# A vision tower's attention phase: scores one eighth of a unit earlier, and features gathered in the first six eighths

## The reference

```
h = einsum('bhid,oi,od->bho', x, weighted_sum, weight)
h = h + attn(layernorm(h))
h = h + ffn(layernorm(h))
```

```
h = ln(x, g1, beta1)
q = elu((h @ wq per head) @ proj) + 1
k = elu((h @ wk per head) @ proj) + 1
v = h @ wv
kv = kv + k_t v_t ; ksum = ksum + k_t        # over tokens
out_t = (q_t . kv) / (q_t . ksum + 1e-6)
x = x + out @ wo ; x = x + mlp(ln(x))
```

## Time and profile before

| | us |
|---|---|
| median of 3 runs | 2545.34 (2538.14 to 2553.37) |
| profiled execution | 2542.18 |
| its span | 2540.4 |
| PE busy | 2215.7 (87%) |
| VectorE busy | 1784.6 (70%) |
| ScalarE busy | 1524.6 (60%) |
| GpSimd busy | 1467.8 (58%) |

### The profile page before, as it was taken

The page is one execution under the profiler, slowest core; times in us unless marked ns, Lnnn a source line. Parts: engine busy times, 40 slices in busy tenths (PEclk is TensorE's granted clock), DMA queues, the critical chain, the costliest instruction groups (busy, mean ns, idle before and its releaser), DMA issues. The chain is left out here.

```text
span 2540.4 us, 64867 instructions
## 1 busy us (share of the span) xinstructions
PE 2215.7 (87%) x24112; PEld 1732.1 (68%) x24112; DVE 1784.6 (70%) x3983; ACT 1524.6 (60%) x2890; POOL 1467.8 (58%) x1449
## 2 busy tenths in 40 slices
PE   3799999999989899999999986799999999994764
PEld 2577777778778777777778775466666666662653
DVE  3477777777777777777777775478788887874443
ACT  3476676676766676667667664556566565651322
POOL 1466666575666666656657654035646555556676
PEclk8899999999999999999999998899999999997897
DMA  3344444344454343434433333111212111100775
GB/s 112 97 119 113 122 123 124 104 131 122 105 132 124 100 105 102 108 99 105 110 101 104 89 87 112 40 60 45 82 43 83 45 60 52 40 22 22 166 139 72
DMA packets 323208, 236.43 MB, mean 93 GB/s; under 512 B 40345, under 2 KB 288141, under 8 KB 322896
## 3 DMA queue, kind: packets, MB, share of 16 engines
q1 hardware_dynamic: 286640, 197.30, 28.6%
q0 software_dynamic: 23808, 21.74, 4.9%
q10 hardware_dynamic: 12448, 13.24, 1.6%
HBM read 73.32 MB, written 82.58 MB: 61 GB/s over the span
## 5 line engine op out<-in xcount | busy, mean ns | idle before, releaser
L965 POOL TENSOR_TENSOR lo<-z,hi 128x512 f16<-128x512 f32 x256 | 306.1, 1196 | 342.8 <-DVE hi L874 328.5
L1850 POOL DMA_INDIRECT slot_dram<-xt,slot_u x256 | 267.0, 1043 | 77.4 <-issue 77.4
L543 PE MATMUL pF<-nh,qk_h 128*128 128x256 f16 x1024 | 282.7, 276 | 7.5 <-DVE nl L862 4.4
L545 PE MATMUL pF<-nl,qk_h 128*128 128x256 f16 x1024 | 282.6, 276 | 0.0
L544 PE MATMUL pF<-nh,qk_l 128*128 128x256 f16 x1024 | 282.6, 276 | 0.0
L789 ACT ACTIVATE sh<-sm 128x512 f16<-128x512 f32 x256 | 159.5, 623 | 106.3 <-DVE sm L895 106.2
L984 POOL TENSOR_TENSOR kvl<-kvacc,kvh 128x260 f16<-128x260 f32 x192 | 157.4, 820 | 77.2 <-ACT kvh L820 77.1
L869 DVE SCALAR_TENSOR_TENSOR z<-pF,z 128x512 f32<-128x512 f32 x256 | 174.9, 683 | 24.6 <-ACT z L772 22.2
L768 ACT ACTIVATE z<-pF 128x512 f32<-128x512 f32 x256 | 150.4, 587 | 69.6 <-PE pF L545 69.6
L543 PE MATMUL pM<-xh,tok_h 128*128 128x256 f16 x512 | 141.3, 276 | 53.9 <-POOL xl L959 53.3
L895 DVE TENSOR_TENSOR sm<-pS,mask 128x512 f32<-128x512 f32 x256 | 174.5, 681 | 17.2 <-PE pS L629 16.9
(11 more groups left out here) (298 smaller groups left out, 8494.2 us busy)
## 6 DMA issues: line engine op xcount, KB each, us to landing
w_w<-in_x SPq DMA_DIRECT2D x128, 256.0 KB, 3.0
qdh<-hi SPq DMA_DIRECT2D x512, 64.0 KB, 2.1
qdl<-lo SPq DMA_DIRECT2D x512, 64.0 KB, 2.1
ks<-hi SPq DMA_DIRECT2D x256, 64.0 KB, 2.1
ks<-lo SPq DMA_DIRECT2D x256, 64.0 KB, 2.1
slot_dram<-blank ACTq DMA_DIRECT2D x8, 1360.0 KB, 7.1
xg<-slot_dram SPq DMA_DIRECT2D x40, 272.0 KB, 3.2
x_dram<-x SPq DMA_DIRECT2D x32, 256.0 KB, 2.4
```

Source lines behind the costliest of these rows:

```text
L543: pe.matmul(out, wh, mh, start=first, stop=False, skip_group_check=True)
L545: return pe.matmul(out, wh, ml, start=False, stop=last, skip_group_check=True)
L965: nc.gpsimd.tensor_tensor(lo[:, n % 2, :, :], z[:, units(w, FEATS, n) % ZS, :, :], hi[:, n % MOVES, :, :], ALU.subtract).then_inc(fl_ready, 1)
L1850: nc.gpsimd.indirect_dma_start(io["slot_dram"], bass.IndirectOffsetOnAxis(slot_u[:, i % XT, c, k:k + 1], 0), xt[:, i % XT, c, :], None, bo ...
```

## The change: the table of dense work and the place of the scores

Each quad is scored one eighth earlier: quads 0, 1, 2 of the next chunk stand at g = 1, 2, 3, and quad 3 of the present chunk at g = 0. Three quads, not two, are scored ahead of the first unit. In the table the features stand in s0, s1, s3, s4, s5 and the values in s6 and s7; the projection stays early in s2. Each inner tuple is an eighth, its first entry early, its second late.

```diff
-DENSE = ((("f", 0),), (("f", 1), ("f", 2)), (("p", 0), ("f", 3)), (("v", 0), ("v", 1)), (("f", 4),),
-         (("f", 5), ("f", 6)), (("f", 7), ("v", 2)), (("v", 3),))
+DENSE = ((("f", 0), ("f", 1)), (("f", 2),), (("p", 0),), (("f", 3), ("f", 4)), (("f", 5),),
+         (("f", 6), ("f", 7)), (("v", 0), ("v", 1)), (("v", 2), ("v", 3)))
...
-                    if g < 2:
-                        quad = (i, c, g + 2)
+
+                    if g == 0:
+                        quad = (i, c, 3)
                     elif c < CH - 1:
-                        quad = (i, c + 1, g - 2)
+                        quad = (i, c + 1, g - 1)
                     else:
-                        quad = None if last else (i + 1, 0, g - 2)
+                        quad = None if last else (i + 1, 0, g - 1)
...
-            for q in range(2):
+            for q in range(3):
                 step("scores", 0, 0, q)
                 step("scores_split", 0, 0, q)
```

## The result

The changed kernel takes 2708.06 us (median of 4 runs, 2706.14 to 2711.91) against 2548.79 for the kernel before (4 runs): ratio 1.0637, 95% interval 1.0614 to 1.0661. The direction was forecast, the size was not: +160 us where +100 was forecast, and the time lies above the range. The profiled execution took 2709.5 us, its span is 2707.8, and 163.5 us of the 167.4 by which the span grew lie between the first scores and the last projection (1465.2 us before, 1628.7 now). What comes behind that point takes 966 us before and 967 after. So the question stays inside the attention phase.

What follows compares the result with a forecast made beforehand. PE's work plus its waits were taken to bound the attention phase. New waits 183 plus 19 minus old waits 132 gave +70; with +30 for the clock, 2542 became 2642 us; 8-in-10 range 2550 to 2700.

Steps and rivals of the forecast that it cites:

- Part one: Before the outputs (pO): scoring quads 1 and 3 two eighths ahead removes all 57.1 us of PE's wait.
- The scores at s7: PE waits for f7 behind SyncE's queue of DMAs: 3.35 us per unit, bounds 0.9 and 4.3.
- mix 0: First mixing group, s4: new wait for xl 0 of 1.9 us every unit; above 2.4 if f3's lo is late.
- mix 2: Mixing group waiting for xl 2 behind f6's lo: new wait 1.25 us in odd halves, 0.1 in even ones.
- Rival A: The scores' wait doesn't grow, since the last feature's own chain decides; faster, 2455 or 2485 us; chance 12%.
- Var and the keys: Waits at var and the keys of s1, 0.3 us each, 19 us over 31 units; each between 0 and 1.4.
- The clock: PE's clock falls behind 18 of 31 waits for the scores, 1.65 us each: +30 us, bounds 0 and 51.
- all 31: Upper bound of the clock cost: a fall behind each of the 31 waits for the scores, 51 us.
- The window of the earlier trace with 0.81: Window around one of PE's longest waits for the scores, granted clock 0.81: that fall cost 1.5 us.
- the old 132: PE's old waits before outputs, mixing, scores and key transposes, 132.0 us, taken away entirely as the most the change can give.
- C: Rival: each of the 31 stalls drops the clock, 2663 us; 2708 with mix 0 and s7 at upper bounds; chance 22%.

Runs made afterwards that it cites:

- e6: The changed kernel with four of the eight DMAs of each query feature left out (scores wrong there); ratio 1.0065.
- e4: The changed kernel with SyncE issuing each input load behind the next feature's DMAs instead of ahead of them; ratio 1.0358.
- e3: The changed kernel with f4 early and f5 late in s4, so no late feature in s3; ratio 1.0627.
- e13: The changed kernel with the first input split of s3 (xh, xl 0, SyncE's load) ahead of GpSimd's sl of quad 2 and kvl; ratio 1.0491.
- after: The changed kernel itself, with both the earlier quads and the new feature table, against the kernel before; 2708.06 us, ratio 1.0637.
- e7: The kernel before (quads where they were) with the new table, but f4 early and f5 late in s4; ratio 0.9981.
- e5: The changed kernel with dummy matmuls filling PE's waits, 24 before the wait for f7 and 16 before mix 0; ratio 1.0540.
- e15: The kernel before with the new table, and in s3 and s7 the scores, their mask and their split moved ahead; ratio 0.9852.
- e1: The changed kernel with the table of before, so the earlier quads alone; ratio 1.0984.
- e8: As e7, with SyncE's input loads behind the next feature's DMAs too; ratio 0.9985.
- e9: The kernel before with the new table, and in s3 and s7 the scores' split ahead of the late dense group; ratio 0.9982.
- e16: The same kernel as e2, run again on another chip; ratio 0.9863.
- e2: The kernel before with the new feature table and the quads where they were; ratio 0.9861.

## Why the prediction was right in direction and wrong in size

**Part one, the outputs' 57 us go: right.** Their idle is 0.0.

**The scores at s7, forecast 3.35 us per unit: right on average, in part by luck.** 104.8 of the 106.7 us are at s7, 3.38 in each of 31 units (in units 6 to 25 3.61 in even and 2.94 in odd halves). But they range from 0.2 to 5.6 us, and not all are longer than the longest before. Each link was later than laid out, and that the errors nearly cancel I had not foreseen: from F3's start (704.58 in the unit shown) f4's first DMA stands at 9.9 (forecast 9.6), SyncE is through at 27.6 (26.4; 0.8 of the difference are f5's hi DMAs, 2.02 instead of 1.25 us), the scores go on at 29.3 (28.1). PE too was later, ready at 26.4 instead of 24.8, since it had waited longer at mix 0 and mix 2. In units 6 to 25 the scores go on 2.0 (even) and 1.5 us (odd) later than laid out, and PE is ready 1.7 and 1.9 us later. e6 shows the cause as forecast, SyncE's queue, and e4 the load in it. Rival A (the last feature's own chain decides) is out.

**Mix 0, forecast 1.9 us: too small, and one link was wrong.** Measured 2.41 in even and 2.20 in odd halves. sh ran where I had put it, 5.4 to 6.0 us behind F3. But GpSimd wasn't free for sl: f3's lo ended, ol stood behind it, and sl began at 6.3 and took 1.37 us, not the 1.16 of the earlier trace rows. e3 (sh without F4 in front: 2.1 and 2.0 left) and e13 (xl ahead of sl: 0.7 and 0.5) show it. I had named f3's lo as the way to the upper bound; that was the case. Mix 2 waited 0.30 and 1.70 (forecast 0.1 and 1.25), since f4 landed 2.0 and 2.4 us behind its last issue, not 1.7. In the phase the mixing has 93.7 where my layout gives 79 (31 x 1.9, 15 x 1.25 and 16 x 0.1). That layout counted it in all 31 units, but the mixing is for the unit three ahead, so 29 have it: 74 us by my own waits. The waits themselves were too small by 20 us, mix 0 by 12 and mix 2 by 8, and the wrong count hid 5 of them.

**Var and the keys, forecast 19: 27.8** (11.7 and 16.1), within their bounds. Smaller groups, the kept-sum outputs and the turn, add 4. So the idle time grew by 102 where 70 was forecast.

**The clock: the step that failed most.** I took 18 falls at 1.65 us, +30, with an upper bound of 51 for "all 31", and counted as candidates only the waits for the scores. The phase has 39 falls where it had 5 before. Of the 36 between 137 and 1660 us, 24 are at waits for the scores and 12 behind waits of the mixing, which are 2.2 to 3.2 us long. PE's busy time rose by 61 us, 1.8 for each of the 34 added. So the price of a fall was right, its number was half of what came, and the bound left out a kind of wait that my own forecast put at 1.9 us. Three stage windows of after, behind mix 0 at 661.4, behind mix 0 at 714.16 and behind the scores at 733.90, show it:

```profile
661.00:669.00 8.00, 7.64 (x88) 6.46 (x89) 5.13 (x11) 3.92 (x8) 5.85 (x7) 0.79 0.44 114
714.00:722.00 8.00, 7.84 (x97) 6.86 (x98) 6.32 (x13) 5.75 (x12) 5.27 (x6) 1.00 0.42 108
733.00:741.00 8.00, 7.10 (x63) 5.23 (x64) 1.89 (x5) 2.61 (x5) 1.51 (x2) 0.79 0.13 40
```

The first two waits are 2.4 and 2.2 us long; the clock fell behind the one and not behind the other. The window of the earlier trace rows with 0.81 was the right price, since 31 of the 39 falls are as short as that one. e7 shows 22 falls with 1.8 us of waiting for the scores in the whole kernel, and e5 that the clock comes back when the waits are filled. A fall should have been weighed for every wait of my layout, not for those of the scores alone.

The Trainium skill (TensorE: Matmul & The Clock Gate, Why this matters for your kernels) has idle gaps of some microseconds throttle the engine. The trace agrees: the clock fell at 20 of the 21 waits for the scores over 3 us. It fell at shorter ones too, at 11 of the 34 waits of the mixing of 2.0 to 2.5 us.

**The sum.** Idle 102 and clock 61 make 163, the growth of the phase; forecast were 70 and 30. Of the 63 us missing, 31 are the clock, 14 the mixing, 9 var and keys, 3 the scores, 4 smaller groups, and 2.5 a wait of the mixing that stands ahead of the phase and stayed, though I took away all of the old 132. So the idle time was as much too small as the clock, but spread over several terms.

**The rivals.** C (each stall drops the clock) gave 2663, and 2708 with both bounds. It is nearest to the time, but its words aren't what happened: the clock fell at 24 of the scores' waits, not 31, and at a dozen of the mixing's, and the scores' wait wasn't at its bound; that 2708 is also the measured time is luck. I had the doubt in the right case and cut the range at 2700.

## What to carry to other kernels

Where a change has two halves, cost each by itself: here one half gained 1.4% and the other cost 10%, and the half that costs is the one that removes the largest wait of the profile. Before work is asked for earlier, follow the data that it needs back to the queue that delivers it (here 24 DMAs in one queue, 17.7 us); a wait of 1.4 us at the consumer was exchanged for one of 3.4 at that queue. And in the sum, every new wait near 2 us or more on TensorE can carry a second price through the clock, here 61 us on 102 us of waiting: count them all, and expect that filling them returns only what the chain behind them lets go.

## What the runs showed of the hardware

- How often TensorE's clock fell, by the length of the wait: at 20 of 21 waits for the scores over 3 us (after); at 10 of 20 waits of the mixing of 2.2 to 2.5 us and 1 of 14 of 2.0 to 2.2 us (after); at none of 29 waits of the mixing of 1.5 to 2.0 us (e15). But in e7 it fell at 14 of 14 waits for the outputs of 2.0 to 2.2 us and at 5 of 16 of 2.2 to 2.5 us. So the length of a wait alone doesn't decide it around 2 us; what else does was not varied.
- GpSimd's sl took 1.15 to 1.17 us everywhere in the kernel before, and in after 1.33 to 1.37 for 62 of 128, nearly all in two places of the unit. It goes by the place, not by the tile: in e13, where xl 0 stands in sl's place in s3, xl 0 takes 1.35 us or more in 28 of 29 units (1.16 at most in after), and sl, now behind it, 1.15 in the unit shown. Which of the work beside it stretches it wasn't varied.
- What comes behind the attention phase, the same instructions in every run, took 965 to 967 us on the chips of e1 to e8 and 1071 to 1078 on those of e9 to e16. A group that differs is the ffn's; e2, and then e16:

```profile
L1302 PE MATMUL pY<-w_h,gh 128*128 128x256 f16 x480 | 130.8, 272 | 0.0
```

```profile
L1302 PE MATMUL pY<-w_h,gh 128*128 128x256 f16 x480 | 145.9, 304 | 20.3 <-issue 19.9
```

Why, no run here shows; a ratio against a kernel timed on another chip would have been off by 4%.
